# Graph attention layer: the accumulators start at zero, are rescaled once a group, and a node's own row is added at the end

## The reference, cut to what matters

```
n = x.shape[0]
loop = jnp.arange(n)
src = jnp.concatenate([edge_index[0], loop])      # every node has an edge to itself
dst = jnp.concatenate([edge_index[1], loop])
h = (x @ W).reshape(n, H, C)
a_src = jnp.einsum('nhc,hc->nh', h, att_src)
a_dst = jnp.einsum('nhc,hc->nh', h, att_dst)
e = a_src[src] + a_dst[dst]
e = jnp.where(e > 0, e, 0.2 * e)
m = jax.ops.segment_max(e, dst, num_segments=n)
ex = jnp.exp(e - m[dst])
denom = jax.ops.segment_sum(ex, dst, num_segments=n)
alpha = ex / denom[dst]
msg = h[src] * alpha[..., None]
out = jax.ops.segment_sum(msg, dst, num_segments=n).reshape(n, H * C) + bias
y = out + x
# then a layer norm of y with ln_w, ln_b, added to the layer's input
```

## Time and profile before

| | before |
|---|---|
| median of 3 runs | 7105.77 us |
| lowest and highest run | 7048.13 and 7116.05 us |
| span of the profiled execution | 7405.0 us |
| the layer's front, until DVE has the sorted records | 0 to 788 us |
| the loop over the groups | 788 to 2105 us |
| block after the loop, until L677 | 2105 to 2188 us |

### The profile page before, as it was taken

How to read it: one execution, slowest core, us unless ns; L and a number is a source line. 1 busy time by engine, 2 the same in 40 slices (tenths; PEclk the granted TensorE clock), 3 DMA queues, 4 the chain that set the end, 5 groups by cost and what they waited for, 6 DMA issues and landing times. The chain is left out here.

```text
span 7405.0 us, 83243 instructions
## 1 busy us (share of the span) xinstructions
PE 4987.3 (67%) x21442; PEld 3487.6 (47%) x21443; DVE 4140.2 (56%) x11930; ACT 2331.7 (31%) x4546; POOL 3609.5 (49%) x3179
## 2 busy tenths in 40 slices
PE   1995477777737966667783677639994555545685
PEld 1663365555525644445552555425662323223474
DVE  9202388888874667774525777773453334433534
ACT  0332244444411223332123555533322222211132
POOL 4777677777742327771034554300007673766043
PEclk9997678877758988888856777759996677766687
DMA  2553344434412255552132222200013332333324
GB/s 52 139 141 74 84 110 112 111 108 109 108 50 69 66 87 165 160 167 64 41 85 77 69 69 68 55 15 9 13 29 93 89 93 63 90 92 88 108 77 105
DMA packets 408552, 630.27 MB, mean 85 GB/s; under 512 B 163019, under 2 KB 290119, under 8 KB 406851
## 3 DMA queue, kind: packets, MB, share of 16 engines
q0 software_dynamic: 180096, 360.11, 18.7%
q1 hardware_dynamic: 227822, 260.35, 13.3%
q10 hardware_dynamic: 308, 6.40, 0.3%
HBM read 470.99 MB, written 154.65 MB: 84 GB/s over the span
## 5 line engine op out<-in xcount | busy, mean ns | idle before, releaser
L779 POOL DMA_INDIRECT conv_rows<-rows_b,index x832 | 843.4, 1014 | 1235.4 <-SPq L2682 884.5
L811 DVE TENSOR_TENSOR acc<-acc,ps 125x257 f32 (+1 forms) x1664 | 701.4, 422 | 930.5 <-DMA acc<-slots,ffn_slot_of 348.8
L2728 PE MATMUL ps<-conv_rows,conv_weight_of 128*125 128x256 f32 x1664 | 633.0, 520 | 599.1 <-issue 297.7
L332 POOL DMA_INDIRECT records_src<-by_src_edge_stage,by_src_edge_slot x400 | 560.0, 1400 | 458.0 <-DMA by_src_edge_stage<-edge_rows 340.4
L2728 PEld LDWEIGHTS ps<-conv_rows,conv_weight_of 128*125 128x125 f32 x1664 | 367.3, 248 | 864.8 <-issue 575.8
L779 POOL DMA_INDIRECT gat_rows<-rows,index x416 | 501.9, 1207 | 256.9 <-PE ps L1089 136.2
L779 POOL DMA_INDIRECT mpnn_rows<-rows_b,index x416 | 472.9, 1137 | 305.3 <-issue 122.1
L496 POOL DMA_INDIRECT records_dst<-front_back,front_dst_addr x400 | 503.6, 1259 | 234.7 <-issue 234.7
L779 POOL DMA_INDIRECT hyp_rows<-rows,index x416 | 417.1, 1003 | 407.8 <-PE ps L2335 274.3
L2716 ACT ACTIVATE conv_weight_of<-conv_onehot_b,index 128x125 f32<-128x125 bf16 x832 | 251.5, 386 | 980.2 <-DVE conv_onehot_b L2700 797.4
L1013 ACT CAST room<-ps 125x1024 bf16<-125x1024 f32 x416 | 409.0, 1016 | 458.3 <-PE ps L1076 374.8
(11 more groups left out here) (582 smaller groups left out, 10558.5 us busy)
## 6 DMA issues: line engine op xcount, KB each, us to landing
mpnn_edge<-records_src SPq DMA_DIRECT2D x104, 512.0 KB
edge_rows<-front_edge_ring SPq DMA_DIRECT2D x100, 451.5 KB
by_src_edge_stage<-edge_rows SPq DMA_DIRECT2D x100, 451.5 KB
conv_rows<-rows_b,index POOLq DMA_INDIRECT x832
front_attr<-in_edge_attr SPq DMA_DIRECT2D x100, 112.0 KB
rows_b<-acc SPq DMA_DIRECT2D x15, 560.0 KB
second_w<-in_L_ffn_w SPq DMA_DIRECT2D x1, 8192.0 KB
slots<-mlp_y SPq DMA_DIRECT2D x56, 128.0 KB
```

Of the source, the lines that this page charges most:

```text
L332: pool.indirect_dma_start(out=self.S.records["src"], out_offset=bass.IndirectOffsetOnAxis(ap=self.addr[:, c:c + 1], axis=0), in_=self.stag ...
L779: pool.indirect_dma_start(out=rows[:, n % U, t, :], out_offset=None, in_=table, in_offset=bass.IndirectOffsetOnAxis(ap=ends[:, n * G + t:n ...
L811: dve.tensor_tensor(here, here, S.ps[0:P, t % banks, 0:width], ALU.add).then_inc(added, 1)
L2728: pe.matmul(S.ps[0:P, t, 0:D], weight_of[:, q.slot, t, :], rows[:, q.slot, t, :], start=True, stop=True).then_inc(summed, 1)
```

## The change

`S.acc` is cleared in `front` once its rows have been stored, so it starts at zero with a denominator of zero. The edges are sorted by block, so within a group only the block of the first tile can hold something from earlier groups: every other block begins inside this group and is still zero. So `add_up` rescales for the tile t = 0 of a group alone. `notfirst`, `first_no` and the semaphore `noted` go, and with them L950.

The edge of a node to itself is left out of the loop. At its start DVE copies e of that edge into `own`. Once the last maxima have been taken, SP loads h of all nodes from `S.rows` again, blocks 0 to 23 into the space that the spreads have used (`own_rows`) and block 24 into `own_last`. Behind the loop `own` becomes exp(e - m), is added to the denominators and multiplied into the loaded rows (25 products), and these are added to `S.acc` (one sum of 24 blocks, one of the last).

```diff
@@ front, vector @@
-                ch.link(dve.tensor_tensor(gat.notfirst[:, 1:], dst.blk[0:P, 1:], dst.blk[0:P, 0:NT - 1], ALU.is_equal))
-                ch.link(dve.memset(gat.notfirst[:].rearrange("p (g t) -> p g t", t=G)[:, :, 0], 0.0))
+                dve.wait_ge(nodes_stored, ROWS_IN)
+                ch.link(dve.memset(S.acc[:], 0.0))
@@ gat, sync @@
                 edges.load(sp, 6 * GROUPS)
+                sp.wait_ge(taken, 2 * GROUPS)
+                h_rows = S.rows.rearrange("(t p) c -> p t c", p=P)[:, :, 0:D]
+                move_rows(sp, own_rows, h_rows[:, 0:NB - 1], own_in)
+                move_rows(sp, own_last, h_rows[:, NB - 1], own_in)
+                sp.wait_ge(own_in, 2 * ROWS_IN)
@@ gat, vector @@
-                ch.step(dve.memset(S.acc[:, :, D:XG], 1.0))
...
                 dve.sem_inc(tables_ready, 1)
+                ch.link(dve.tensor_copy(own[:], at_start))
@@ raise_tables @@
-                    dve.tensor_copy(first_no[:, now], notfirst[:, q.tiles()]).then_inc(noted, 1)
@@ add_up @@
-                            dve.wait_ge(noted, q.n + 1)
                         for t, b in zip(tiles, blocks):
                             if q.tile_since(t, 1):
                                 dve.wait_ge(added, q.n * G + t)
-                            here = S.acc[:, bass.ds(b, 1), :].rearrange("p a (c h) -> p (a c) h", h=HEADS)
-                            by = factor[:, par, bass.ds(b, 1), :].to_broadcast([P, HC + 1, HEADS])
-                            dve.scalar_tensor_tensor(here, by, first_no[:, par, t:t + 1], here, ALU.max, ALU.mult)\
-                               .then_inc(rescaled, 1)
-                            dve.wait_ge(rescaled, q.n * G + t + 1)
+                            if t == 0:
+                                here = S.acc[:, bass.ds(b, 1), :].rearrange("p a (c h) -> p (a c) h", h=HEADS)
+                                by = factor[:, par, bass.ds(b, 1), :].to_broadcast([P, HC + 1, HEADS])
+                                dve.scalar_tensor_tensor(here, by, 0.0, here, ALU.max, ALU.mult).then_inc(rescaled, 1)
+                                dve.wait_ge(rescaled, q.n + 1)
@@ block after the loop, scalar @@
+                act.wait_ge(own_ready, 1)
+                act.activation(own[:], own[:], ACT.Exp).then_inc(own_weighed, 1)
                 act.wait_ge(var_ready, 1)
@@ block after the loop, vector @@
-                ch.link(dve.reciprocal(inv_sum[:], S.acc[:, :, D:XG]))
+                ch.link(dve.tensor_tensor(own[:], own[:], node[:, (GROUPS - 1) % 2, :, HEADS:], ALU.subtract))
+                dve.sem_inc(own_ready, 1)
+                dve.wait_ge(own_weighed, 1)
+                ch.link(dve.tensor_tensor(inv_sum[:], S.acc[:, :, D:XG], own[:], ALU.add))
+                ch.link(dve.reciprocal(inv_sum[:], inv_sum[:]))
                 v = S.acc[:, :, 0:D].rearrange("p t (c h) -> p t c h", h=HEADS)
+                mine = [own_rows[:, t] for t in range(NB - 1)] + [own_last[:]]
+                for t in range(NB):
+                    m = mine[t].rearrange("p (c h) -> p c h", h=HEADS)
+                    ch.step(dve.tensor_tensor(m, m, bc_mid(own[:, t, :], HC), ALU.mult))
+                ch.sync()
+                ch.step(dve.tensor_tensor(S.acc[:, 0:NB - 1, 0:D], S.acc[:, 0:NB - 1, 0:D], own_rows, ALU.add))
+                ch.link(dve.tensor_tensor(S.acc[:, NB - 1, 0:D], S.acc[:, NB - 1, 0:D], own_last[:], ALU.add))
```

More of the change, by code:

```diff
@@ L860, in attention_tables @@
     t.node, t.most = sb("gat_node", [P, 2, NB, 2 * HEADS]), sb("gat_most", [P, NB, HEADS])
-    t.notfirst = sb("gat_notfirst", [P, NT], BF16)
+    t.own = sb("gat_own", [P, NB, HEADS])
     return t
@@ L872, in gat @@
     bias, ln_w, ln_b = tables.bias, tables.ln_w, tables.ln_b
-    node, most, notfirst = tables.node, tables.most, tables.notfirst
+    node, most, own = tables.node, tables.most, tables.own
     with phase(nc, "gat") as (sb, sem):
+        own_last, own_in = sb("own_last", [P, D]), sem("own_in")
+        own_rows = S.xT[0:P].rearrange("p k n -> p (k n)")[:, 0:(NB - 1) * D].rearrange("p (t d) -> p t d", d=D)
         dve_step = sem("dve_step")
@@ L879, in gat @@
             sem(x) for x in ("go", "tables_ready", "selected", "turned", "opened", "widened", "others", "rounded"))
-        spread, evacuated, halving, taken, merged, tabling, tabled, risen, factored, noted = (
+        spread, evacuated, halving, taken, merged, tabling, tabled, risen, factored = (
             sem(x) for x in ("spread", "evacuated", "halving", "taken", "merged", "tabling", "tabled", "risen",
-                             "factored", "noted"))
+                             "factored"))
         looked_up, scoring, shifted, weighted, scaled, summed, rescaled, added = (
@@ L894, in gat @@
             red, rise = mb("red", [P, 2, H, HEADS]), mb("rise", [P, NB, HEADS])
-            factor, first_no = mb("factor", [P, 2, NB, HEADS]), mb("first_no", [P, 2, G])
+            factor = mb("factor", [P, 2, NB, HEADS])
             score = mb("score", [128, 2, G, HEADS])
@@ L1125, in gat @@
         var_ready, root_ready = sem("var_ready"), sem("root_ready")
+        own_ready, own_weighed = sem("own_ready"), sem("own_weighed")
         with nc.Block() as block, ExitStack() as ctx:
```

## The result

| | before | after |
|---|---|---|
| median | 7104.38 us (4 runs, 7048.13 to 7116.05) | 7003.78 us (4 runs, 7001.43 to 7008.68) |
| ratio, 95% interval | | 0.9864, 0.9831 to 0.9897 |
| span of the profiled execution | 7405.0 us | 6999.7 us |

The account below looks back on a forecast made before the run. DVE was taken to bound the loop at 24.2 us a group, the others close behind. Loop -103, start +0.2 and block behind the loop +14 gave -89 us: 7017 us from 7105.8, range 6950 to 7065.

Parts of the forecast that it names:

- DVE sets the pace before: Loop over 52 groups: DVE, in its own order, sets the 24.2 us a group, with the other engines close behind.
- POOL's floor, taken as 21.8 us: Loop: POOL's eight gathers and six scatters need between 20.1 and 22.1 us a group; 21.8 taken.
- DVE with PE, 24.2 - 2.2 = 22.0 us: Loop: without seven rescales a group, tiles 0 to 3 win 0.5 us, tiles 4 to 7 1.6, the L950 copy 0.1.
- Two limits near each other, combined to 22.2: Loop: limits of 22.0 and 21.8 us don't overlap perfectly, so 22.2 us a group, 2.0 won over 49 groups: 98 us.
- the fast rival: Loop: POOL and PE both loosen, 21.0 us a group (sign: under 21.5), 6957 us in all; chance 0.15.
- The chances: Whole kernel: 0.68 below 7034.7 us, from nine tenths of the forecast (0.58), the fast rival and most of the late load (0.05).
- The hand-over rival: Loop: PE's slow sums and wider-spaced adds leave 1.1 us won a group, 7062 us in all; chance 0.17.
- POOL's stalls beside the rescales: Loop: by the shared-port rule, 364 vanishing locks would lower POOL's floor by 0.5 us a group, at best 24 us more.
- Own rows' load hidden: End of the loop: SP's 3.2 MB load takes 19 us under some 23 us of cover, 4 us to spare.
- Front free: Front: clearing the accumulator takes 5.56 us inside DVE's 109.40 us of idle time and doesn't hold up POOL; cost 0.
- The block behind the loop, +14: After the loop: 17 us of added DVE work, less 3 us because two more POOL scatters get out early.

Follow-up runs that it names:

- e4_before_five: Kernel before the change with POOL issuing five scatters a group instead of six, the rest issued later: 7415.0 us, 0.9995 of the kernel before in its series.
- c4_four: Changed kernel with POOL issuing four scatters a group instead of six, 104 moved to later stages: 6957.62 us, 0.9789 of the kernel before.
- e0_before: Kernel before the change, unchanged, profiled again: 7103.52 us, profile span 7101.8 us, period 23.80 us a group.
- c1_after: The changed kernel itself, run again in a later series: 7000.35 us, 0.9849 of the kernel before.
- c3_one_input: Changed kernel with a one-SBUF-input product by 1.0 added on the blocks of tiles 1 to 3: 7007.99 us, 0.9859 of the kernel before.
- e2_all_rescales: The change with its own rows and cleared accumulator, but the rescale of every tile kept: 7103.96 us, 0.9983 of the kernel before.
- e6_one_input: Same kernel as `c3_one_input`, run in the disturbed second series: 7429.27 us, 1.0011 of the kernel before.

## Why the prediction was right, point by point

**DVE sets the pace before:** right. `e4_before_five` leaves POOL a scatter less, and POOL waits instead.

**POOL's floor, taken as 21.8 us:** right, 21.7. The runs of after show it as the period itself. It falls 0.3 us from the 22.0 of before. That it was hit within 0.15 us is in part luck: the value was picked between 20.1 and 22.1, and this width is worth 98 us. The mean gather issue went from 1218 to 1049 ns, the mean scatter issue from 1337 to 1510: most of the stall moved from gathers to scatters.

**DVE with PE, 24.2 - 2.2 = 22.0 us:** this is the step that failed in size. `c4_four` shows 20.6, from 23.8: 3.2 us won, not 2.2. Of the 1.4 us between 22.0 and 20.6 this makes 1.0; the other 0.4 is the slower loop of the profile that the prediction started from (24.20 against 23.80), which it had taken as it stood. The adds of the second half took 4.48 us from the first rescale to the last add's end in the mean of 40 groups of `e0_before`, and 2.46 in `c4_four`: 2.0 won against the 1.6 taken. Those of the first half went from 4.83 to 3.99, 0.84 against 0.5. Both came out at the faster of the two ends that the prediction had worked out (2.85 with L950), where I had taken a value near the middle. The timeline of a second half in `c4_four`:

```profile
1448.82 1.00 DVE L1001 TENSOR_TENSOR acc<-acc,ps 125x264 f32 x2
1450.23 1.00 DVE L1001 TENSOR_TENSOR acc<-acc,ps 125x264 f32 x2 [0.41 <-PE ps L1094]
```

The price of a bare add was also less than the 0.63 us read from the convolution's loop: two in 1.00 us, so 0.57 apart.

**Two limits near each other, combined to 22.2:** wrong through the step before. With 20.6 beside 21.65 nothing has to be added, and the period is POOL's 21.65. The forecast of 2.0 us won a group came close to the measured 2.15 because POOL's floor, the better of the two estimates, capped the other, and because two errors cancelled: the period was put 0.55 us too high, 22.2 for 21.65, and the one it was subtracted from 0.4 too high. That is luck. From the undisturbed 23.80 the same 22.2 would have won only 1.6. The forecast named 22.2 and called anything under 21.5 the fast rival; 21.65 lies between, in the forecast's own range of 21.6 to 22.7. The fast rival had the right view of PE (its look-up below) and the wrong one of POOL.

**The chances:** the parts named for less than 7034.7 us, 0.52, 0.15 and most of 0.05, come to 0.71, not the 0.68 written.

**The hand-over rival:** its sign came, adds waiting for PE 121.0 us against 13.8 in the earlier trace rows, but its price did not. In after that wait is the end of the chain from POOL's late gathers, by ACT and PE; where POOL is relieved (`c4_four`) it is still 97.1 us, and the period is 20.6.

**POOL's stalls beside the rescales,** left to the range: by the table above they were 18.1 us in 40 groups, 0.45 us a group, and are gone. One of them in `e0_before`, a scatter issue of 1.44 us that starts inside a rescale:

```profile
1421.89 0.49 DVE L991 SCALAR_TENSOR_TENSOR acc<-gat_factor,gat_first_no,acc  x1 [0.18 <-DVE acc L996]
...
1422.04 1.44 POOL L332 DMA_INDIRECT records_src<-by_src_edge_stage,by_src_edge_slot  x1 [0.30 <-issue]
```

The Trainium skill (SBUF — State Buffer, section on the two separate sides) says that a DVE operation with two SBUF inputs holds the port pair that GpSimd shares, against a GpSimd operation that reads SBUF. The trace agrees: the scatter above took 1.44 us against 1.19. The estimate that the prediction made by that rule, 0.5 us a group, agrees with the 0.45 measured, but only as a product: 3.6 issues a group started in a rescale where it had counted 2.0, and each was held 0.13 us where it had counted 0.25. The effect of these stalls on the time was smaller, 0.3 to 0.4 us a group, since the remaining issues met the long operations elsewhere (3.1 us of stall a group before, 2.8 after).

**Own rows' load hidden:** right. SP issues it from 1928.13 on. The share of the DMA engines in 40 slices from 1925 to 1960 us, in tenths:

```profile
DMA  0000369999999999999997100000005898998000
```

Its transfer ends after 23 slices of 0.875 us, at 1945; the last add ends at 1950.2, and DVE goes on at 1950.52 without a wait for SP. 5 us were left where 4 were forecast.

**Front free:** right. The clearing takes place while DVE would idle, and POOL's scatter beside it takes 1.19 us:

```profile
699.66 5.56 DVE L647 MEMSET acc<- 125x6600 f32 x1 [24.88 <-issue]
700.13 1.19 POOL L496 DMA_INDIRECT records_dst<-front_back,front_dst_addr  x1 [0.30 <-issue]
...
782.40 0.43 DVE L650 CAST index<-front_back 128x416 int32<-128x416 f32 x1 [77.18 <-DMA front_back<-records_dst]
```

**The block behind the loop, +14:** +10.7. DVE and POOL there, in after:

```profile
1953.22 8.14 DVE L1165 TENSOR_TENSOR room<-room,attention_gat_own 125x256 f32<-125x256 f32 x24
...
1961.73 6.56 DVE L1167 TENSOR_TENSOR acc<-acc,room 125x6144 f32<-125x6144 f32 x1
...
1968.66 8.50 DVE L1170 TENSOR_TENSOR acc<-acc,attention_gat_most 125x256 f32<-125x256 f32 x25
...
2043.78 1.40 DVE L677 BATCH_NORM_STATS2 ln_stats<-room 125x6 f32<-125x256 f32 x4 [5.94 <-PEq L93]
```

```profile
1955.72 7.03 POOL L332 DMA_INDIRECT records_src<-by_src_edge_stage,by_src_edge_slot  x1 [46.13 <-DMA by_src_edge_stage<-edge_rows]
1963.06 6.29 POOL L332 DMA_INDIRECT records_src<-by_src_edge_stage,by_src_edge_slot  x1 [0.30 <-issue]
1969.66 1.19 POOL L332 DMA_INDIRECT records_src<-by_src_edge_stage,by_src_edge_slot  x1 [0.30 <-issue]
1971.15 1.37 POOL L332 DMA_INDIRECT records_src<-by_src_edge_stage,by_src_edge_slot  x1 [0.30 <-issue]
...
2032.34 6.57 POOL L332 DMA_INDIRECT records_src<-by_src_edge_stage,by_src_edge_slot  x1 [0.30 <-issue]
```

DVE's added work is 16.7 us, 17 forecast (products 8.14 + 0.43, sums 6.56 + 0.42). POOL's tail shrank by 6.0, not 3: DVE's idle time before L677 was 12.00 us in `e0_before` and is 5.94. The forecast left two scatters to be issued behind DVE's end; none was left, and the last one, started before, ends at 2038.91, 1.1 us behind DVE. The mis-sized term is the number that gets out early: besides the two in the added stretches, two more got through under the 25 short products L1170. In `c1_after`, the same kernel in another execution, the block took 89.2 us, so this term itself varies by 4 us.

## What to carry to other kernels

Work out, for each engine that runs a loop in a fixed order, what its own instructions need in a group without any waiting, and forecast with the largest of these after the edit: here the engine that came second, POOL with 22.0 us of 23.8, decided what a saving of 3.2 us on DVE was worth. The quickest proof of which one it is, is to take a little work from the suspected one in both kernels; it moved one by 0.93 us a group, in the other POOL waited 1.44 us a group longer instead, and it pointed to a version that is faster than both. Before two traces are subtracted, or a limit read from one is set beside another, compare each span with the median of its kernel's runs; where the runs of a kernel fall into groups, look at the stages outside the change first.

## What the runs showed of the hardware that was not expected

- The same two-input operations can shorten a loop that POOL limits. Three more of 0.43 us a group on DVE took the period from 21.61 to 21.13 us, because POOL's issues then started beside long operations less often.
- An indirect issue of POOL is held by a DVE operation with two SBUF inputs only if it starts while that runs, and then until about its end (0.7 to 2.1 us beside L983 of 2.28 us). What it overlaps later costs it nothing.
- A DVE product of a block with 1.0 (`c3_one_input`, one SBUF input, 125x264 elements in 0.30 us) is held itself: where it started when half to four fifths of a POOL issue was over, it lasted to about 0.1 us behind the issue's end, up to 0.73 us (33 of 156). The two-input operations of 0.43 us never took more than 0.50.
- A row of such operations without a gap holds an issue in one place and lets it through in another. Beside the products L1165 it took 7.03 us, beside the 25 of L1170 two took 1.19 and 1.37 us and the third 5.40. The traces don't show what decides.
- A rescale with an immediate in place of a scalar for each partition took 427 ns against 493 for the same 125x264 elements, with 0.0 in the place of `first_no`.
- PE's look-up was faster where less idle time stood before it: its 16 products took 346 ns each in the mean behind 175.4 us of idle time in `e0_before` (780 to 2110 us), and 261 ns behind 4.9 us in after. The granted clock between 900 and 1850 us was 0.79 and 0.83 of full speed. In `c4_four`, with the idle time back (134.1 us in 900 to 1850), it was 306 ns.
- A later layer ran at a granted clock of 0.50 in `e0_before` and of 1.00 in `e2_all_rescales`, 712 and 456 ns for the same product: 56 us, more than half of what the change wins.
- In one series the kernel before took 7422 us instead of 7109. The profiles of that series show idle times whose releaser is given as outside the core, up to 11.9 us in `e6_one_input`, in a program on one core.
